# A mixer and mixture-of-experts kernel on one core: the final stage's roots of expert rows in two rounds of 8 and 24 tiles, and a new order of weighing and normalising

## The chip, the core and the metric

One core of a Trainium2 chip. The metric is device time in microseconds (us) of one execution, as the median of several runs; lower is better. The kernel before took 280.55 us in the median of 3 runs (280.05 to 281.44). Something the size of 0.5% (1.4 us) is about what a measurement of this kernel can tell from no change.

## The reference

The input x has 4096 tokens of 128 numbers. A gated state-space mixer and a layer norm come first; they lie outside the change. Then comes a mixture of 8 experts of which each token uses two, and a last layer norm:

```python
scores = xt @ gate_w
ew, ei = jax.lax.top_k(scores, K)          # K = 2
ew = jax.nn.softmax(ew, axis=-1)
h = gelu(einsum('td,edf->etf', xt, w1) + b1)
o = einsum('etf,efd->etd', h, w2) + b2
y = _layernorm(xt + o, ln_g, ln_b)         # per expert: (r - mean) * rsqrt(var + 1e-6) * g + b
out = einsum('et,etd->td', wE, y)          # two experts per token, with softmax weights
x = _layernorm(x + out)                    # eps 1e-5
```

## The kernel before

**Up to the final stage.** The kernel is written out by hand: each engine has its own instruction stream, and semaphores join them. After the mixer and the routing, every token is copied to the buckets of its two experts in device memory. 18 batches of 4 expert tiles go through TensorE, ScalarE (GELU) and VectorE. A row that leaves this part is (r - mean) * g with its mean and variance in two further columns (130 numbers), not yet multiplied by the root of the variance. GpSimd scatters the rows to `y_rows`, two per token.

**The final stage** starts when all scatters have landed. It handles 32 tiles of 128 tokens, in 8 groups of 4 tiles (g0 to g7), one PSUM bank for each group; two groups are a round (`ROUNDS` = 4, `OT` = 8 tiles). Its work on each engine is as follows.

- SP loads the expert rows of each group from `y_rows` into `yin` (L420; eight loads of 520 KB, all issued one after the other; the semaphore `yin_in[r]` is for round r). At the end it stores groups of the output as they become ready, g7 before g6 (L425).
- TensorE first adds up in each bank what needs no expert rows: the token itself (L778) and the weighted bias of the norm (L779), for all 8 groups. Then it adds, group by group in order, the token's first expert row (L783, two instructions in the profile of 512 columns; waits for `t0_ready`, which ScalarE gives for every 4 tiles) and its second expert row (L788, 8 instructions in the profile for 4 tiles of 128 columns; waits for `t1_ready`, which VectorE gives per tile). `sums_ready` counts the groups.
- VectorE `scales(r)`: the roots of the variances of a round, by shifts and three Newton steps, each of its 13 instructions waiting for the one before (`root_steps`): L1396, L1036, L1039, three times L1043, L1046, L1049, and L1401, which writes `scale`. A round has 8 tiles of 2 rows, so each instruction has 16 columns.
- VectorE `weigh_second(r)`: 8 multiplications of a 128x128 tile (L1411). ScalarE `weigh_first(r)`: the same for the first rows (L981). Both wait for the roots of their round.
- VectorE `second_statistics(r)`: 8 instructions that read the banks (L1420); wait for `sums_ready`.
- VectorE `second_norm_scales(r)`: the last norm's roots of a round, a chain of 14 steps and two closing instructions (L1013 to L1022, L1036 to L1049, L1433, L1434), 8 columns wide; gives `norm2_ready`.
- ScalarE `normalise_out(r)`: 8 tiles of the output (L989), waits for `norm2_ready`; of the last round it does 4 tiles and VectorE the other 4 (L1461).

**The order** on VectorE is written out by generators: one chain's next step is issued between two steps of another, so that its wait for its own predecessor is filled. It is `scales(0)` alone; `weigh_second(0)` with `scales(1)` between its tiles; the rest of `scales(1)`; `weigh_second(1)`; `second_statistics(0)`. Then, for r = 0 to 3, `second_norm_scales(r)` leads, and beside it run in this order `scales(r + 2)`, `weigh_second(r + 2)`, `second_statistics(r + 1)`, as far as these exist; what is left of them is issued behind. On ScalarE the order is `weigh_first` 0, 1, 2, `normalise_out(0)`, `weigh_first(3)`, `normalise_out` 1, 2, 3.

Of the kernel before, what the change touches and what calls it, by code (L numbers as in the profile page):

```python
# [2 lines left out]

# [6 lines left out]
ALU = mybir.AluOpType  # L10
# [3 lines left out]
P = 128  # L14
# [9 lines left out]
ROOT_STEPS = 13  # L24
# [43 lines left out]
def alone(steps):  # L68


    for _ in steps:
        pass


def later(k, n):

    return not isinstance(k, int) or k >= n


def mixer_moe_kernel(nc, x, W_u, b_u, W_g, b_g, A, Bm, Cm, D, gate_w, w1, b1, w2, b2, ln_g, ln_b, out):  # L80
# [16 lines left out]
    TOP = 2  # L97
# [7 lines left out]
    YW = DIM + 2  # L105
# [7 lines left out]
    ROUNDS = GROUPS // 2  # L113
    OT = 2 * TPG
# [14 lines left out]
    with ExitStack() as ctx:  # L129
        def sb(name, shape, dt=F32):  # L130
            return ctx.enter_context(nc.sbuf_tensor(name, shape, dt))

        def sem(name):
            return ctx.enter_context(nc.semaphore(name))
# [23 lines left out]
        rows = sb("rows", [ROWS, P])  # L158
# [29 lines left out]
        yin = by_token[:, 0:YIN].rearrange("p (a c) -> p a c", c=YW)  # L188
# [16 lines left out]
        weight = sb("weight", [P, TOP, GROUPS * TPG])  # L205
# [18 lines left out]
        zt = [z1T[i][:, 0:2 * P].rearrange("p (s d) -> p s d", d=P) for i in range(2)]  # L224
        stz = sb("stz", [P, BT, 6])
        yb = [powers_then_yb[:, i * BT * YW:(i + 1) * BT * YW].rearrange("p (s c) -> p s c", c=YW) for i in range(NB)]
        tmpz = sb("tmpz", [P, 6, OT * TOP])
        row_ids = [sb(f"row_ids{i}", [P, BT], I32) for i in range(NB)]
        tmp2 = sb("tmp2", [P, 6, OT])
        scale = sb("scale", [P, GROUPS * TPG, TOP])  # L230
# [71 lines left out]
        yin_in = [sem(f"yin_in{i}") for i in range(ROUNDS)]  # L302
        b2_steps = sem("b2_steps")
        root_steps = sem("root_steps")
# [14 lines left out]
        def block_of(s):  # L319

            return slice(s * P, (s + 1) * P)
# [471 lines left out]
        def _(act):  # L793
# [180 lines left out]

            def weigh_first(r):

                act.wait_ge(root_steps, (r + 1) * ROOT_STEPS)
                for j in range(OT):
                    t = r * OT + j
                    row = yin[:, t * TOP, 0:P]  # L980
                    ins = f(row, row, ACT.Copy, scale=scale[:, t, 0:1])  # L981
                    if j % TPG == TPG - 1:
                        ins.then_inc(t0_ready, 1)

            def normalise_out(r, tiles=OT):
                act.wait_ge(norm2_ready, r + 1)
                for j in range(tiles):
                    t = r * OT + j
                    ins = f(out_rows[:, t, :], bank[t // TPG][:, block_of(t % TPG)], ACT.Identity,  # L989
                            bias=nb2[:, t:t + 1], scale=rstd2[:, t:t + 1])  # L990
                    if j % TPG == TPG - 1:
                        ins.then_inc(out_ready, 1)

            weigh_first(0)
            weigh_first(1)
            for r in range(ROUNDS - 2):
                weigh_first(r + 2)
                normalise_out(r)
            normalise_out(ROUNDS - 2)
            normalise_out(ROUNDS - 1, TPG)  # L1000


# [1 line left out]
        def _(dve):  # L1004
            v = nc.vector
            cp, tt, ts, stt = v.tensor_copy, v.tensor_tensor, v.tensor_scalar, v.scalar_tensor_tensor

            def variance(steps, st, tmp, q, n, eps):

                me, mo, qe, qo = st[:, 0:n, 1], st[:, 0:n, 4], st[:, 0:n, 2], st[:, 0:n, 5]  # L1010
                d, dd = tmp[:, 0, 0:n], tmp[:, 2, 0:n]
                steps.wait()
                steps.step(tt(d, me, mo, ALU.subtract))  # L1013
                steps.step(tt(half_sums(tmp, n), me, mo, ALU.add))
                steps.step(tt(q, qe, qo, ALU.add))
                yield
                steps.wait()
                steps.step(stt(dd, d, 0.25, d, ALU.mult, ALU.mult))
                steps.step(ts(q, q, 1.0 / P, eps, ALU.mult, ALU.add))
                yield  # L1020
                steps.wait()
                steps.step(tt(q, q, dd, ALU.add))  # L1022
                yield

            def half_sums(tmp, n):
                return tmp[:, 1, 0:n]

            def root(tmp, n):
                return tmp[:, 5, 0:n]

            def rsqrt(steps, q, tmp, n):

                a, y = tmp[:, 4, 0:n], root(tmp, n)
                yi = y.bitcast(I32)
                steps.wait()
                steps.step(ts(yi, q.bitcast(I32), 1, None, ALU.logical_shift_right))  # L1036
                yield
                steps.wait()
                steps.step(ts(yi, yi, -1.0, float(RSQRT_MAGIC), ALU.mult, ALU.add))  # L1039
                yield  # L1040
                for _ in range(3):
                    steps.wait()
                    steps.step(tt(a, y, y, ALU.mult))  # L1043
                    yield
                    steps.wait()
                    steps.step(stt(a, a, -0.5, q, ALU.mult, ALU.mult))  # L1046
                    yield
                    steps.wait()
                    steps.step(stt(y, a, 1.5, y, ALU.add, ALU.mult))  # L1049
                    yield  # L1050
# [166 lines left out]
            rows_now, tiles, upto, one, taken_step, later_skip = (cnt[:, i, :] for i in range(6))  # L1217
# [170 lines left out]

            roots = Counted(dve, root_steps, ROOT_STEPS)

            def scales(r):

                dve.wait_ge(yin_in[r], 32)
                roots.open(r)
                roots.wait()
                roots.step(ts(tmpz[:, 3, :], yin[:, bass.ds(r * OT * TOP, OT * TOP), P + 1:YW]  # L1396
                              .rearrange("p j a -> p (j a)"), EPS_MOE, None, ALU.add))
                yield
                yield from rsqrt(roots, tmpz[:, 3, :], tmpz, OT * TOP)
                roots.wait()  # L1400
                roots.step(tt(scale[:, bass.ds(r * OT, OT), :], root(tmpz, OT * TOP).rearrange("p (j k) -> p j k", k=TOP),  # L1401
                              weight[:, :, bass.ds(r * OT, OT)].rearrange("p k j -> p j k"), ALU.mult))
                roots.close()

            def weigh_second(r):

                dve.wait_ge(root_steps, (r + 1) * ROOT_STEPS)
                for j in range(OT):
                    t = r * OT + j
                    row = yin[:, t * TOP + 1, 0:P]  # L1410
                    ts(row, row, scale[:, t, 1:2], None, ALU.mult).then_inc(t1_ready, 1)  # L1411
                    yield

            def second_statistics(r):
                if later(r, 1):
                    dve.wait_ge(out_steps, (r - 1) * OUT_STEPS + 3)
                for j in range(OT):
                    if j % TPG == 0:
                        dve.wait_ge(sums_ready, r * (OT // TPG) + j // TPG + 1)
                    ins = v.bn_stats(st2[:, j, :], bank[r * (OT // TPG) + j // TPG][:, block_of(j % TPG)])  # L1420
                    if j == OT - 1:
                        ins.then_inc(stats2_ready, 1)
                    yield

            def second_norm_scales(r):
                late.open(r)
                dve.wait_ge(stats2_ready, r + 1)
                if later(r, 1):
                    dve.wait_ge(norm2_ready, r)
                yield from variance(late, st2, tmp2, tmp2[:, 3, :], OT, EPS1)  # L1430
                yield from rsqrt(late, tmp2[:, 3, :], tmp2, OT)
                late.wait()
                late.step(cp(rstd2[:, bass.ds(r * OT, OT)], root(tmp2, OT)))  # L1433
                stt(nb2[:, bass.ds(r * OT, OT)], half_sums(tmp2, OT), -0.5, root(tmp2, OT), ALU.mult, ALU.mult)\  # L1434
                    .then_inc(norm2_ready, 1)
                late.close()

            alone(scales(0))
            second_scales = scales(1)
            for _ in weigh_second(0):  # L1440
                next(second_scales, None)
            alone(second_scales)
            alone(weigh_second(1))
            alone(second_statistics(0))
            for r in range(ROUNDS):


                beside = []
                if r + 2 < ROUNDS:
                    beside.append(scales(r + 2))  # L1450
                    beside.append(weigh_second(r + 2))
                if r + 1 < ROUNDS:
                    beside.append(second_statistics(r + 1))
                beside = chain(*beside)
                for _ in second_norm_scales(r):
                    next(beside, None)
                alone(beside)

            dve.wait_ge(norm2_ready, ROUNDS)
            for t in range((GROUPS - 1) * TPG, GROUPS * TPG):  # L1460
# [98 lines left out]
```

## Time and profile before

| | us |
|---|---|
| median of 3 runs | 280.55 |
| lowest, highest | 280.05, 281.44 |
| the profiled execution's own time | 280.12 |
| its span in the profile | 278.3 |
| TensorE matmul busy | 224.3 (81%) |
| VectorE busy | 173.6 (62%) |
| GpSimd busy | 139.8 (50%) |
| ScalarE busy | 137.7 (49%) |

All times of a trace count from the start of the span. The profiled execution took 1.82 us more than its span. A row of the timeline gives the start, the duration, the engine, the line in the kernel, what is written and read with the shapes, and how many instructions are merged in it; in brackets stands the idle time before it and who ended it. A row of merged instructions has the time from the first start to the last end. TensorE's granted clock (PEclk) is a share of 2.4 GHz: 1.00 is 2.4 GHz and 0.50 is 1.2 GHz. Idle time of an engine costs something only where the end of the kernel hangs on it, which the chain of waits shows.

### The profile page before, as it was taken

The page shows a single profiled execution, that of the slowest core. Times are in us where ns is not written, and L with a number is a line of the kernel's source. Part 1 is how long each engine was busy: PE and PEld are TensorE (multiplying, and loading weights), DVE is VectorE, ACT ScalarE, POOL GpSimd, SP SyncE. Part 2 cuts the span into 40 slices and gives each one's busy share as a digit, 9 for nine tenths or more (in the row PEclk, how much of TensorE's full clock was granted, in tenths as well). Part 3 has the DMA queues.
Part 4 walks back from the last instruction along what each step waited for, and adds up shares of the span by engine and source line. Part 5 has one row for each costly group of instructions (what it writes and reads, how often), then busy time and mean ns, then how long its engine had stood idle before and what let it go on. Part 6 is the DMA issues. An engine that isn't in the chain of part 4 may idle for free.

```text
span 278.3 us, 5571 instructions
## 1 busy us (share of the span) xinstructions
PE 224.3 (81%) x1316; PEld 169.5 (61%) x1317; DVE 173.6 (62%) x913; ACT 137.7 (49%) x404; POOL 139.8 (50%) x179
## 2 busy tenths in 40 slices
PE   3998998996798356447999999999999938997640
PEld 2476864664655335346888888888888823455330
DVE  1245527787628769475666676766666680569974
ACT  2242223667500304547667767776876500244844
POOL 7000000477777577777777777777777773000000
PEclk9999999999799777555999999999999986999895
DMA  5990000011111111644343333333232111940224
GB/s 170 293 273 14 0 0 1 21 50 61 48 57 38 38 58 55 150 103 117 86 106 98 102 102 107 84 107 96 81 93 64 58 38 33 419 164 1 75 75 151
DMA packets 22375, 25.66 MB, mean 92 GB/s; under 512 B 4388, under 2 KB 16569, under 8 KB 22348
## 3 DMA queue, kind: packets, MB, share of 16 engines
q1 hardware_dynamic: 17958, 16.84, 20.7%
q0 software_dynamic: 4352, 8.50, 9.2%
q8 instruction: 10, 0.16, 0.2%
q14 instruction: 17, 0.14, 0.2%
q10 hardware_dynamic: 38, 0.01, 0.0%
HBM read 14.15 MB, written 11.71 MB: 93 GB/s over the span
## 4 chain that ended last, share of the span: by engine, by line
PE 65%; DVE 21%; ACT 7%; issue 2%; DMA 1%; ACTq 1%; DVEq 0%
PE bank L721 14%; PE bank L731 13%; PE bank L733 4%; PE bank L455 3%; PE bank L778 3%; PE bank L456 3%; PE bank L779 3%; PE bank L474 3%; PE bank L706 3%; ACT pay L828 2%; PE bank L524 2%; PE bank L547 2%; PE bank L517 2%; PE bank L446 2%; PE bank L783 2%
## 5 line engine op out<-in xcount | busy, mean ns | idle before, releaser
L1516 POOL DMA_INDIRECT buckets<-pay,dest x64 | 63.2, 988 | 67.2 <-ACT pay L828 50.4
L1524 POOL DMA_INDIRECT y_rows<-powers_then_yb,row_ids x72 | 71.1, 987 | 24.5 <-issue 18.6
L731 PE MATMUL bank<-w_sb,hidden 128*128 x288 | 48.2, 290 | 0.0
L927 ACT ACTIVATE hidden<-bank,bcol 128x128 f32<-128x128 f32 x144 | 40.9, 371 | 9.7 <-PE bank L721 9.6
L721 PE MATMUL bank<-xbT,x_tok 128*128 128x128 f32 x288 | 44.1, 300 | 1.4 <-ACT xbT L909 1.4
L731 PEld LDWEIGHTS bank<-w_sb,hidden 128*128 128x128 f32 x288 | 38.1, 193 | 2.5
L721 PEld LDWEIGHTS bank<-xbT,x_tok 128*128 128x128 f32 x288 | 37.2, 202 | 4.0 <-ACT xbT L909 1.8
L917 ACT ACTIVATE x_tok<-w_sb 128x256 f32 x72 | 26.4, 432 | 0.7 <-issue 0.7
L1364 DVE SCALAR_TENSOR_TENSOR powers_then_yb<-z1T,powers_then_yb,gbc 128x128 f32<-128x128 f32 x72 | 22.2, 350 | 5.5 <-DVE powers_then_yb L1360 0.7
L828 ACT ACTIVATE pay<-z,nb,tmp 128x128 f32<-128x128 f32 x32 | 13.1, 484 | 24.2 <-DVE nb L1141 24.2
L1352 DVE TENSOR_TENSOR z1T<-bank,gates_then_xb 128x256 f32<-128x256 f32 x36 | 15.2, 421 | 13.0 <-PE bank L733 13.0
L981 ACT ACTIVATE by_token<-by_token,scale 128x128 f32<-128x128 f32 x32 | 9.8, 388 | 19.6 <-DVE scale L1401 19.6
L474 PE MATMUL bank<-by_token,powers_then_yb 128*128 128x128 f32 x60 | 14.3, 323 | 6.1 <-ACT by_token L817 4.2
L909 ACT ACTIVATE xbT<-bank 128x512 f32<-128x512 f32 x18 | 10.8, 599 | 16.8 <-PE bank L706 16.8
L1356 DVE BATCH_NORM_STATS2 stz<-z1T 128x6 f32<-128x128 f32 x72 | 17.5, 285 | 1.2
L733 PE MATMUL bank<-b_parts,ones 3*128 x72 | 16.2, 225 | 0.0
L474 PEld LDWEIGHTS bank<-by_token,powers_then_yb 128*128 128x128 f32 x60 | 9.8, 201 | 10.3 <-ACT by_token L817 6.8
L555 PE MATMUL bank<-chosen,before 128*128 128x32 bf16 x8 | 1.6, 197 | 17.5 <-DVE chosen L1189 17.5
L800 ACT ACTIVATE gates_then_xb<-bank,bcol 128x512 f32<-128x512 f32 x8 | 5.5, 687 | 17.5 <-PE bank L455 17.5
L547 PE MATMUL bank<-cat,z1T 128*128 128x136 f32 x64 | 12.2, 348 | 1.6 <-DVE z1T L1127 1.6
L547 PEld LDWEIGHTS bank<-cat,z1T 128*128 128x128 f32 x64 | 10.7, 242 | 4.0 <-DVE z1T L1127 3.0
L783 PE MATMUL bank<-by_token,cat 128*128 128x512 f32 x16 | 9.3, 668 | 4.6 <-ACT by_token L981 4.6
(187 smaller groups left out, 409.4 us busy)
## 6 DMA issues: line engine op xcount, KB each, us to landing
gates_then_xb<-buckets SPq DMA_DIRECT2D x72, 64.5 KB
by_token<-y_rows SPq DMA_DIRECT2D x8, 520.0 KB, 6.6
x_tok<-in_L_attn_x_dram SPq DMA_DIRECT2D x8, 256.0 KB, 5.5
out_dram<-out_rows SPq DMA_DIRECT2D x8, 256.0 KB, 2.5
y_rows<-powers_then_yb,row_ids POOLq DMA_INDIRECT x72, 2.3
w_sb<-in_L_ffn_w_dram SPq DMA_DIRECT2D x1, 1024.0 KB
buckets<-pay,dest POOLq DMA_INDIRECT x64, 2.3
buckets<-pad SPq DMA_DIRECT2D x9, 64.5 KB, 2.6
```

What stands on the lines that cost most here:

```text
L474: mm(ps_state[s % 2][:, 0:P], pq[:, 0, 1, :], local[h][:, block_of(s - 1)], start=False, stop=True).then_inc(state_product[h], 1)
L547: ins = mm(ps_tok[j // 2][:, c:c + CW], z1T[g % 2][:, block_of(j)], cat[:], start=True, stop=True)
L721: ins = mm(ps_hid[(q % 2) * 2 + h][:, at:at + P], w1_now[q][:, s, c * P:(c + 1) * P], xbT[q % 2][:, s, :], start=True, stop=True)
L731: mm(ps_o[h][:, i * P:(i + 1) * P], hidden[q % 2][:, s, c, :], w2_sb[:, bass.ds(e * (FC * P) + c * P, P)], start=(c == 0), stop=False)
L733: ins = mm(ps_o[h][:, i * P:(i + 1) * P], ones[0:PARTS, :], b2_parts[:, bass.ds(e * P, P)], start=False, stop=True)
L828: f(pay[0][:, g * TPG + j, 0:P], z1[g % 2][:, j, 0:P], ACT.Identity, bias=nb1[g % 2][:, j:j + 1], scale=tmp1[g % 2][:, 5, j:j + 1]).then_i ...
L917: ins = f(w1_now[q][:, s, :], w1_sb[:, bass.ds(e[s] * HID, HID)], ACT.Copy)
L927: ins = f(hidden[q % 2][:, s, c, :], ps_hid[(q % 2) * 2 + s // 2][:, at:at + P], ACT.Gelu, bias=bcol[:, bass.ds(e[s] * FC + BIAS_ROW + c, 1)])
L1356: ins = v.bn_stats(stz[:, s, :], buf[:, s - 2 * h, :])
L1364: stt(y[:, s, 0:P], buf[:, s - 2 * h, :], y[:, s, P:P + 1], gbc[:, bass.ds(e[s] * P, P)], ALU.subtract, ALU.mult).then_inc(yb_ready, 1)
L1516: pool.indirect_dma_start(buckets, bass.IndirectOffsetOnAxis(ap=dest[:, k, t:t + 1], axis=0), pay[k][:, t, :], None).then_inc(scattered[g ...
L1524: pool.indirect_dma_start(y_rows, bass.IndirectOffsetOnAxis(ap=row_ids[q][:, s:s + 1], axis=0), yb[q][:, s, :], None, bounds_check=TOKENS ...
```

## The change

On VectorE the roots of expert rows are made in two rounds: `scales(0, 0, 1)` for the first 8 tiles (16 columns), and `scales(1, 1, ROUNDS)` for the other 24 (48 columns), which waits for the loads of rounds 1 to 3 together. The second one leads, and `second_norm_scales(0)` runs beside it. So `weigh_second(1)` and the roots of round 1 come after `second_statistics(0)` instead of ahead of it, and `weigh_second(0)` has nothing beside it. `weigh_second(3)` runs beside `second_norm_scales(1)`, and `second_statistics(3)` beside `second_norm_scales(2)`, while `second_statistics` 1 and 2 stand alone.

On ScalarE the list is now written differently: `weigh_first` 0, 1, 2, `normalise_out(0)`, `weigh_first(3)`, `normalise_out` 1, 2, 3: `ROUNDS - 1` is 3, so it is the order of before, while `weigh_first` 1, 2 and 3 now all wait for the second round of roots. In detail:

```diff
--- before.py
+++ after.py
@@ -1,5 +1,4 @@
-from itertools import chain
...
@@ -224,7 +223,7 @@
         zt = [z1T[i][:, 0:2 * P].rearrange("p (s d) -> p s d", d=P) for i in range(2)]
         stz = sb("stz", [P, BT, 6])
         yb = [powers_then_yb[:, i * BT * YW:(i + 1) * BT * YW].rearrange("p (s c) -> p s c", c=YW) for i in range(NB)]
-        tmpz = sb("tmpz", [P, 6, OT * TOP])
+        tmpz = sb("tmpz", [P, 6, (ROUNDS - 1) * OT * TOP])
         row_ids = [sb(f"row_ids{i}", [P, BT], I32) for i in range(NB)]
         tmp2 = sb("tmp2", [P, 6, OT])
         scale = sb("scale", [P, GROUPS * TPG, TOP])
@@ -974,7 +973,7 @@
 
             def weigh_first(r):
 
-                act.wait_ge(root_steps, (r + 1) * ROOT_STEPS)
+                act.wait_ge(root_steps, min(r + 1, 2) * ROOT_STEPS)
                 for j in range(OT):
                     t = r * OT + j
                     row = yin[:, t * TOP, 0:P]
@@ -991,12 +990,12 @@
                     if j % TPG == TPG - 1:
                         ins.then_inc(out_ready, 1)
 
-            weigh_first(0)
-            weigh_first(1)
-            for r in range(ROUNDS - 2):
-                weigh_first(r + 2)
+            for r in range(ROUNDS - 1):
+                weigh_first(r)
+            normalise_out(0)
+            weigh_first(ROUNDS - 1)
+            for r in range(1, ROUNDS - 1):
                 normalise_out(r)
-            normalise_out(ROUNDS - 2)
             normalise_out(ROUNDS - 1, TPG)
 
 
@@ -1388,23 +1387,25 @@
 
             roots = Counted(dve, root_steps, ROOT_STEPS)
 
-            def scales(r):
-
-                dve.wait_ge(yin_in[r], 32)
-                roots.open(r)
+            def scales(n, first, last):
+
+                for r in range(first, last):
+                    dve.wait_ge(yin_in[r], 32)
+                tiles, rows = slice(first * OT, last * OT), (last - first) * OT * TOP
+                roots.open(n)
                 roots.wait()
-                roots.step(ts(tmpz[:, 3, :], yin[:, bass.ds(r * OT * TOP, OT * TOP), P + 1:YW]
+                roots.step(ts(tmpz[:, 3, 0:rows], yin[:, first * OT * TOP:last * OT * TOP, P + 1:YW]
                               .rearrange("p j a -> p (j a)"), EPS_MOE, None, ALU.add))
                 yield
-                yield from rsqrt(roots, tmpz[:, 3, :], tmpz, OT * TOP)
+                yield from rsqrt(roots, tmpz[:, 3, 0:rows], tmpz, rows)
                 roots.wait()
-                roots.step(tt(scale[:, bass.ds(r * OT, OT), :], root(tmpz, OT * TOP).rearrange("p (j k) -> p j k", k=TOP),
-                              weight[:, :, bass.ds(r * OT, OT)].rearrange("p k j -> p j k"), ALU.mult))
+                roots.step(tt(scale[:, tiles, :], root(tmpz, rows).rearrange("p (j k) -> p j k", k=TOP),
+                              weight[:, :, tiles].rearrange("p k j -> p j k"), ALU.mult))
                 roots.close()
 
             def weigh_second(r):
 
-                dve.wait_ge(root_steps, (r + 1) * ROOT_STEPS)
+                dve.wait_ge(root_steps, min(r + 1, 2) * ROOT_STEPS)
                 for j in range(OT):
                     t = r * OT + j
                     row = yin[:, t * TOP + 1, 0:P]
@@ -1435,26 +1436,22 @@
                     .then_inc(norm2_ready, 1)
                 late.close()
 
-            alone(scales(0))
-            second_scales = scales(1)
-            for _ in weigh_second(0):
-                next(second_scales, None)
-            alone(second_scales)
-            alone(weigh_second(1))
-            alone(second_statistics(0))
-            for r in range(ROUNDS):
-
-
-                beside = []
-                if r + 2 < ROUNDS:
-                    beside.append(scales(r + 2))
-                    beside.append(weigh_second(r + 2))
-                if r + 1 < ROUNDS:
-                    beside.append(second_statistics(r + 1))
-                beside = chain(*beside)
-                for _ in second_norm_scales(r):
+            def together(leading, beside):
+                for _ in leading:
                     next(beside, None)
                 alone(beside)
+
+            alone(scales(0, 0, 1))
+            alone(weigh_second(0))
+            alone(second_statistics(0))
+            together(scales(1, 1, ROUNDS), second_norm_scales(0))
+            alone(weigh_second(1))
+            alone(weigh_second(2))
+            alone(second_statistics(1))
+            together(second_norm_scales(1), weigh_second(3))
+            alone(second_statistics(2))
+            together(second_norm_scales(2), second_statistics(3))
+            alone(second_norm_scales(3))
 
             dve.wait_ge(norm2_ready, ROUNDS)
             for t in range((GROUPS - 1) * TPG, GROUPS * TPG):
```

## Rows read from the trace of the kernel before

**Rows 1.** The profile page, section 4: shares of the chain that ended last.
```profile
PE 65%; DVE 21%; ACT 7%; issue 2%; DMA 1%; ACTq 1%; DVEq 0%
```

**Rows 2.** Chain of waits: start us, us, engine, output, line, count.
```profile
260.64 1.28 ACT by_token L981 x4
...
261.97 2.08 PE bank L783 x2
264.05 1.41 PE bank L788 x8
...
266.31 0.91 PE bank L788 x8
```

**Rows 3.** Timeline of VectorE before 251 us: start, us, line, shapes, [idle before].
```profile
239.26 0.17 DVE L1396 TENSOR_SCALAR tmpz<-by_token 128x16 f32<-128x16 f32 x1 [9.50 <-DMA by_token<-y_rows]
...
245.37 1.66 DVE L1411 TENSOR_SCALAR by_token<-by_token,scale 128x128 f32<-128x128 f32 x8
248.39 0.89 DVE L1420 BATCH_NORM_STATS2 st<-bank 128x6 f32<-128x128 f32 x4 [1.35 <-PE bank L788]
```

**Rows 4.** Timeline of VectorE from 251 us on.
```profile
251.06 0.17 DVE L1013 TENSOR_TENSOR tmp<-st 128x8 f32<-128x8 f32 x1
...
253.88 0.17 DVE L1401 TENSOR_TENSOR scale<-tmpz,weight 128x16 f32<-128x16 f32 x1
...
254.64 0.16 DVE L1434 SCALAR_TENSOR_TENSOR nb<-tmp 128x8 f32<-128x8 f32 x1
...
262.44 1.67 DVE L1420 BATCH_NORM_STATS2 st<-bank 128x6 f32<-128x128 f32 x8
...
265.56 0.30 DVE L1420 BATCH_NORM_STATS2 st<-bank 128x6 f32<-128x128 f32 x1 [1.07 <-PE bank L788]
...
267.24 0.30 DVE L1420 BATCH_NORM_STATS2 st<-bank 128x6 f32<-128x128 f32 x1 [0.42 <-PE bank L788]
...
268.07 0.29 DVE L1420 BATCH_NORM_STATS2 st<-bank 128x6 f32<-128x128 f32 x1
...
269.54 0.16 DVE L1434 SCALAR_TENSOR_TENSOR nb<-tmp 128x8 f32<-128x8 f32 x1
...
273.13 1.36 DVE L1461 TENSOR_SCALAR out_rows<-bank,rstd,nb 128x128 f32<-128x128 f32 x4
```

**Rows 5.** The two SP rows of the loads: timeline, and time from issue to landing.
```profile
234.34 3.83 SPq L420 DMA_DIRECT2D by_token<-y_rows  x8
...
DMA to landing us min/median/max: 3.6/6.6/9.7
```

**Rows 6.** Groups of VectorE instructions by shape: busy us, mean ns of one, idle.
```profile
L1204 DVE TENSOR_TENSOR sel<-picked,sel 128x32 f32<-128x32 f32 x16 | 2.4, 190 | 0.3
...
L1043 DVE TENSOR_TENSOR tmpz<-tmpz 128x16 f32<-128x16 f32 x12 | 2.1, 174 | 0.1
```

**Rows 7.** Timeline of TensorE, final stage.
```profile
249.05 1.05 PE L788 MATMUL bank<-by_token,cat 128*128 128x128 f32 x8
...
255.43 1.13 PE L783 MATMUL bank<-by_token,cat 128*128 128x512 f32 x2 [1.82 <-ACT by_token L981]
...
258.14 1.05 PE L788 MATMUL bank<-by_token,cat 128*128 128x128 f32 x8
```

**Rows 8.** Busy by stretch: from:to, length, each engine's busy us, PEclk, DMA, GB/s.
```profile
261.60:261.80 0.20, 0.00 (x0) 0.00 (x0) 0.20 (x2) 0.20 (x2) 0.00 (x0) 0.50 0.00 0
...
264.50:265.00 0.50, 0.50 (x4) 0.50 (x4) 0.00 (x0) 0.50 (x2) 0.00 (x0) 0.50 0.00 0
265.00:265.50 0.50, 0.50 (x5) 0.48 (x5) 0.00 (x0) 0.50 (x3) 0.00 (x0) 0.99 0.34 131
...
271.00:272.00 1.00, 0.00 (x0) 0.00 (x0) 0.83 (x6) 1.00 (x4) 0.00 (x0) 0.92 0.00 0
```

**Rows 9.** Timeline of ScalarE, final stage.
```profile
245.37 2.45 ACT L981 ACTIVATE by_token<-by_token,scale 128x128 f32<-128x128 f32 x8 [0.95 <-DVE scale L1401]
...
256.45 2.87 ACT L989 ACTIVATE out_rows<-bank,nb,rstd 128x128 f32<-128x128 f32 x8
```

## The prediction

> **What bounds the kernel now.** The page comes first: the chain that ended last is 65% TensorE and 21% VectorE [rows 1]. The change touches only what follows the last expert batch, so I read the chain of waits from there on. It shows a stage in which three engines take turns: ScalarE weighs four tiles, TensorE adds g6 and g7, VectorE takes their statistics and makes the roots [rows 2]. The timelines then give the price of each turn. VectorE waits for the first loads until 239.26, and works from 251.06 to 273.13 with two short idles of 1.07 and 0.42 us, both for TensorE [rows 3, 4]. So after 251 us the end hangs on VectorE's own list, and on TensorE where it is late. Ahead of 251.06 VectorE has room: TensorE is still adding what needs no expert rows, and VectorE idles 1.35 us before the first statistics [rows 3].
>
> **Up to 251.06: nothing gained or lost.** The first roots start at the same 239.26. The second round of roots (13 instructions) and 8 weighings leave this stretch. They lay in front of the idle of 1.35 us, which gets longer; `second_statistics(0)` waits for TensorE's g0 and g1, and g1 ends at 250.10 (249.05 + 1.05) either way [rows 3, 7]. This takes work out of a hole and puts it where VectorE is the bound.
>
> **The wait for all loads** costs nothing: the eight are issued by 238.17 and the slowest takes 9.7 us to land, so all are there before 248, three microseconds ahead of the first instruction that waits [rows 5]. SP's stores keep their order, and nothing else is queued on SP behind them. GpSimd has nothing here.
>
> **The wide roots, 251.06 to 254.3.** Before, 13 steps of 16 columns beside a norm chain took 2.99 us (251.06 to 253.88 + 0.17) [rows 4]. No row has this operation at 48 columns. The nearest: 190 ns at 32 columns and 174 at 16 [rows 6], so 16 ns for 16 columns and 32 for the 32 added. Bounds are 0 (the link's latency hides it) and 0.1 us each (three times the slope). I take 0.03: 13 x 0.03 = 0.4. The roots lead now instead of coming after the first three norm instructions, which gives back about 0.1. They end at 251.06 + 2.99 + 0.4 - 0.1 = 254.3 (253.9 to 255.3 by the bounds). The norm chain beside them ends 0.9 us behind the roots' last start before (254.80 against 253.88) [rows 4], so near 255.0 now; VectorE can begin to weigh at 254.8, between its last steps.
>
> **Round 1's turn, the term that decides.** ScalarE starts round 1 at 254.3 instead of in the early hole (245.37) [rows 9]. Four tiles take 1.28 [rows 2], so TensorE can start g2 at 255.6. It had finished g1 at 250.10: it stands idle 5.5 us. In the run before it went on with g2 and g3 at once. What does it do after an idle? After 1.82 us it ran at full clock [rows 7]. After the end of g5 at 259.19 the granted clock was 0.50 from 261.6 on, 2.4 us later, and g6 ran at half clock, 2.08 + 1.41 = 3.49 us; it was back at 0.99 from 265.0 [rows 2, 7, 8]. After the last matmul of all, at 267.2, the fall came inside 271 to 272 us (mean 0.92), so 4.6 us later [rows 8]. An idle of 5.5 us is longer than both, so I take half clock for g2, at the price of g6: 3.49, and then 1.77 for g3 at full clock (as g7, 265.45 to 267.22) [rows 2]. g3 ends at 255.6 + 3.49 + 1.77 = 260.9. VectorE takes its 4 statistics in 0.04 + 0.89 [rows 3] and is done at 261.8.
>
> The Trainium skill, page TensorE: Matmul & The Clock Gate, Part 1, says that the number of slow matmuls at a kernel's start differs from run to run of the same kernel. By it the time would lie anywhere between those of the first two rivals, 280.6 and 284.1; one trace of one execution can't confirm it.
>
> **VectorE's own list meanwhile**: 16 weighings from 254.8 at 1.66 for 8 [rows 3] until 258.1, then 8 statistics of 1.70 [rows 4] until 259.8, if TensorE were never late. So the half clock costs 2.0 us here. The move of round 1 alone is covered by what the change saves elsewhere, as the next rival shows.
>
> **The rest, from 261.8.**
> - Norm chain 1 with `weigh_second(3)` beside it. A chain alone takes 3.43 (269.70 to 273.13, at 0.20 a step); with a tile of 128 columns beside a step the pair takes 0.28 (267.24 to 268.07 is three pairs) [rows 4]. 3.43 + 8 x 0.08 = 4.07. The other reading is norm chain 2 before: 264.11 to 269.70 less the idles 1.07 and 0.42 is 4.10, and the idles hide a little more. I take 4.0 (3.8 to 4.2): 265.8.
> - `second_statistics(2)` alone, 1.70: 267.5. TensorE has had g4 and g5 since 264.5 (260.9 + two times 1.77), so there is no wait.
> - Norm chain 2 with the last statistics, 4.0: 271.5. Those need g6 and g7: ScalarE weighs rounds 1 and 2, normalises round 0 and weighs g6 by 254.3 + 2 x 2.45 + 2.87 + 1.28 = 263.4 [rows 2, 9], before TensorE is free at 264.5, so g7 ends near 268.0. Its first statistic is due at about 268.9. The two idles of before are gone.
> - Norm chain 3 alone, 3.43: 274.9, where it was 273.13.
> - The tail (four tiles on each engine, and the stores of g7 and g6) is the same work in the same spacing; it moves as a whole.
>
> **ScalarE** is no bound: its work from 254.3 is three weighings of 2.45, three normalisings of 2.87 and half of one, 17.4 us, so it could be done at 271.7, and it starts its last half at 274.9.
>
> **The sum.** 274.9 - 273.13 = +1.8 us. The profiled execution took 280.12, so 281.9; the median is 0.43 above it, so 282.3.
>
> **Rivals.**
> - *Not slower: TensorE is at full clock for g2, or its slow stretch is hidden.* Then g3 ends at 255.6 + 2 x 1.77 = 259.1, its statistics at 260.0, and 4.0 + 1.7 + 4.0 + 3.43 behind it give 273.2: +0.1, 280.6. It decides if the clock is still full when g2 starts at 255.6. For it speaks the clock that held for 4.6 us after the last matmul; against it the 5.5 us, and the fall after 2.4. Here also belongs a smaller price of the list (wide roots free, chains at 3.8), with a half-length slow stretch. Together 0.27.
> - *The half clock lasts through g2 and g3.* Both at twice 1.77 take 7.1: g3 ends at 262.7 instead of 260.9: +3.6, 284.1. The one slow stretch near it in the trace ended 3.0 us after TensorE's start (261.97 to 265.0), less than this needs; 0.13.
> - *Faster: VectorE is bound by the number of its instructions.* After 251.06 there are 13 fewer root instructions (26 become 13): 13 x 0.174 = 2.26 saved, plus 1.49 of idle that goes; against it 1.66 for `weigh_second(1)` and 0.4 for the width. -1.7 with TensorE never late: 278.9. Against it: norm chain 0 with 13 roots beside it took 3.74 (251.06 to 254.80), only 0.3 more than a chain alone [rows 4], so the roots lay in gaps and their removal saves 0.3 a round. 0.07. The Trainium skill, page VectorE: DVE Perf Modes, section on the TRN2 errata, would have it this way: a fixed cost for each instruction from SBUF, so few wide ones are cheaper than many narrow ones. The rows agree on the cost of one (174 ns for 16 columns, 190 for 32) and not on what it is worth here.
>
> **How the numbers follow.** My case has 0.53, with its own range 281.2 to 283.2: about 0.40 of it lies above 281.95 (0.5% over the median), 0.13 within. The long half clock adds 0.13 to slower. The first rival's 0.27 goes to same (0.25) but for 0.02 above the bound, and the third is faster. So slower is 0.40 + 0.13 + 0.02 = 0.55, same 0.13 + 0.25 = 0.38, faster 0.07. The likeliest time is 282.3. The range runs from the full-clock case less a few tenths for the free width (280.3) to the long half clock (284.0).
>
> **What would show it in the profile.** Idle of VectorE ahead of the first statistics near 4.7 us instead of 1.35; the wide roots at about 0.20 us each, ending at 254.3; the granted clock at 0.50 when g2 starts at 255.6, and VectorE idle for TensorE before the statistics of g2 and g3, together about 2 us; no idle before the last statistics; the last norm chain alone at 3.43 ending near 274.9. The prediction is wrong if the clock is full at 255.6, if the roots end after 255.3, or if a norm chain with eight tiles beside it takes well under 3.8.

## The result, and the profile after

The changed kernel took 285.49 us in the median of 4 runs (283.80 to 286.06); the kernel before took 281.0 beside it (280.05 to 282.60). The ratio is 1.0183, 95% interval 1.0126 to 1.0239: slower, by more than the 282.3 forecast and outside its range of 280.3 to 284.0. A second comparison of the unedited kernel, in the first experiment below, gave 1.0131 (1.0078 to 1.0185). The ratios leave out executions more than 1.5% above the fastest of their kernel, the medians do not.

| | before | after |
|---|---|---|
| the profiled execution's own time | 280.12 | 283.80 |
| its span | 278.3 | 282.1 |
| first root instruction starts | 239.26 | 240.28 |
| last four tiles on VectorE start | 273.13 | 276.91 |
| between them, "the stage" below | 33.87 | 36.63 |
| VectorE busy | 173.6 | 171.4 |

VectorE is busy 2.2 us less (26 instructions fewer) and the end comes later. The timeline of VectorE in the kernel after has the rows that answer to [rows 3, 4]:

```profile
240.28 0.17 DVE L1397 TENSOR_SCALAR tmpz<-by_token 128x16 f32<-128x16 f32 x1 [9.78 <-DMA by_token<-y_rows]
...
249.16 0.89 DVE L1421 BATCH_NORM_STATS2 st<-bank 128x6 f32<-128x128 f32 x4 [4.50 <-PE bank L787]
250.91 0.89 DVE L1421 BATCH_NORM_STATS2 st<-bank 128x6 f32<-128x128 f32 x4 [0.86 <-PE bank L787]
251.72 0.18 DVE L1397 TENSOR_SCALAR tmpz<-by_token 128x48 f32<-128x48 f32 x1
...
254.75 0.21 DVE L1402 TENSOR_TENSOR scale<-tmpz,weight 128x48 f32<-128x48 f32 x1
...
255.43 3.22 DVE L1412 TENSOR_SCALAR by_token<-by_token,scale 128x128 f32<-128x128 f32 x16
260.21 0.89 DVE L1421 BATCH_NORM_STATS2 st<-bank 128x6 f32<-128x128 f32 x4 [1.56 <-PE bank L787]
263.07 0.89 DVE L1421 BATCH_NORM_STATS2 st<-bank 128x6 f32<-128x128 f32 x4 [1.97 <-PE bank L787]
264.00 0.17 DVE L1012 TENSOR_TENSOR tmp<-st 128x8 f32<-128x8 f32 x1
...
267.78 1.67 DVE L1421 BATCH_NORM_STATS2 st<-bank 128x6 f32<-128x128 f32 x8
269.49 0.17 DVE L1012 TENSOR_TENSOR tmp<-st 128x8 f32<-128x8 f32 x1
...
273.32 0.16 DVE L1435 SCALAR_TENSOR_TENSOR nb<-tmp 128x8 f32<-128x8 f32 x1
```

The two idles of 1.07 and 0.42 us before the last statistics are gone. In their place stand 1.56 and 1.97 us before those of g2 and g3. What VectorE waits for there is TensorE; its timeline (compare [rows 7]), and the busy table by stretch around its slow part (columns as in [rows 8]):

```profile
249.81 1.05 PE L787 MATMUL bank<-by_token,cat 128*128 128x128 f32 x8
256.33 2.07 PE L782 MATMUL bank<-by_token,cat 128*128 128x512 f32 x2 [5.46 <-ACT by_token L980]
258.19 1.91 PE L787 MATMUL bank<-by_token,cat 128*128 128x128 f32 x8
259.90 1.92 PE L782 MATMUL bank<-by_token,cat 128*128 128x512 f32 x2
261.61 1.43 PE L787 MATMUL bank<-by_token,cat 128*128 128x128 f32 x8
262.87 1.02 PE L782 MATMUL bank<-by_token,cat 128*128 128x512 f32 x2
```

```profile
255.25:255.50 0.25, 0.00 (x0) 0.00 (x0) 0.22 (x3) 0.25 (x2) 0.00 (x0) 1.00 0.00 0
255.50:255.75 0.25, 0.00 (x0) 0.00 (x0) 0.25 (x3) 0.25 (x2) 0.00 (x0) 0.61 0.00 0
...
262.00:262.25 0.25, 0.25 (x4) 0.25 (x2) 0.00 (x0) 0.25 (x2) 0.00 (x0) 0.50 0.79 303
262.25:262.50 0.25, 0.25 (x3) 0.25 (x3) 0.00 (x0) 0.25 (x2) 0.00 (x0) 0.73 1.03 393
```

TensorE stood idle for 5.46 us. The granted clock fell to 1.2 GHz near 255.55 (mean 0.61 in the quarter of a microsecond from 255.50), 0.8 us before g2 could start, and came back near 262.4. So g2 (to 260.1, by the chain of waits) and nearly all of g3 (to 263.05) ran at half clock: 6.72 us for the two, where two groups at full clock take 3.5.

Behind the first statistics (from 251.06 before, 251.72 after) the last tiles come 22.07 and 25.19 us later: +3.12. VectorE's waits for TensorE make 2.04 of it (1.56 + 1.97 against 1.07 + 0.42), and its own list is 1.08 longer.

### The profile page after: what moved, and what is told of

It is laid out like the page before. It is cut to its first block, busy times and chain, and to the rows that moved or that the text cites. A ratio compares the mean times of both kernels' runs of the same rounds, so it can differ in the third digit from the quotient of the medians.

```text
span 282.1 us, 5542 instructions
## 1 busy us (share of the span) xinstructions
PE 223.9 (79%) x1314; PEld 168.8 (60%) x1317; DVE 171.4 (61%) x887; ACT 137.4 (49%) x404; POOL 140.2 (50%) x179
## 3 DMA queue, kind: packets, MB, share of 16 engines
HBM read 14.15 MB, written 11.71 MB: 92 GB/s over the span
## 4 chain that ended last, share of the span: by engine, by line
PE 65%; DVE 22%; ACT 7%; issue 3%; DMA 1%; ACTq 1%; DVEq 0%
PE bank L720 13%; PE bank L730 13%; PE bank L732 4%; PE bank L454 3%; PE bank L777 3%; PE bank L473 3%; PE bank L455 3%; PE bank L778 3%; PE bank L705 2%; ACT pay L827 2%; PE bank L523 2%; PE bank L782 2%; PE bank L546 2%; PE bank L516 2%; PE bank L787 2%
## 5 line engine op out<-in xcount | busy, mean ns | idle before, releaser
L782 PE MATMUL bank<-by_token,cat 128*128 128x512 f32 x16 | 10.1, 720 | 5.5 <-ACT by_token L980 5.5
L988 ACT ACTIVATE out_rows<-bank,nb,rstd 128x128 f32<-128x128 f32 x28 | 10.2, 461 | 6.2 <-DVE nb L1435 6.2
```

## The experiments

Theory A: the time is TensorE at half clock after the idle. Theory B: it is VectorE's own list, longer by the wide roots and the order. The stage of each kernel, from the traces. Its start hangs on the landing of the loads and the first statistics on TensorE, so its first part varies: 11.44 and 11.78 us in the two traces of the changed kernel, 11.80 and 11.71 in those of the kernel before. The next column leaves that part out: it counts from the end of the first statistics to the last four tiles.

| kernel | median us | ratio to before (95%) | stage us | behind the first statistics, us | half clock beside g2 to g7, us |
|---|---|---|---|---|---|
| before, its two traces | 281.0 to 281.8 | 1 | 33.87, 33.83 | 22.07, 22.12 | 3.4 (g6) |
| changed, its two traces | 285.49, 285.03 | 1.018, 1.013 | 36.63, 36.98 | 25.19, 25.20 | 6.8 (g2, g3) |
| e2_after_filled | 281.85 | 0.9998 (0.9959 to 1.0037) | 33.80 | 22.29 | none |
| f2_after_half_filled | 283.69 | 1.0122 (1.0067 to 1.0176) | 36.42 | 25.21 | 6.8 |
| g1_after_bridge | 282.99 | 1.0040 (1.0002 to 1.0079) | 35.38 | 23.58 | 3.4 (g2) |
| f4_late_narrow | 285.24 | 1.0134 (1.0086 to 1.0183) | 36.51 | 24.95 | 6.8 |
| e4_before_filled | 279.03 | 0.9886 (0.9828 to 0.9944) | 32.32 | 20.63 | none |
| e3_round1_back | 278.97 | 0.9901 (0.9868 to 0.9934) | 31.60 | 19.74 | none |
| f3_round1_back_early_fill | 277.64 | 0.9786 (0.9711 to 0.9861) | 29.80 | 19.75 | none |

### The changed kernel again (e1_after_again)

No edit.

> The changed kernel once more, unedited, in five rounds. Theory A (half clock: TensorE idles 5.5 us before g2 and then runs g2 and most of g3 at 1.2 GHz): again slower by 4 to 5.5 us, with the granted clock at 0.50 when g2 starts and VectorE idle before the statistics of g2 and g3 for 1.5 to 3.5 us; executions with a lower mean clock are the longer ones. Theory B (VectorE's own list is longer, by the wide roots and the new order): slower by the same in all executions, whatever the mean clock.

Measured: slower by 1.31%, 3.7 us (4 to 5.5 was expected); the traced execution had the same picture: idles of 1.56 and 1.96 us before the statistics of g2 and g3, and half clock from 256.3 to 263.1. The mean clock of the six executions lies between 0.887 and 0.898 and the shortest two (283.31, 283.75) have 0.898, the longest (286.11) 0.887. That goes with A but does not tell it from B: the executions of the kernel before show the same (279.15 us at 0.920, the four of 284.00 to 284.75 at 0.883 to 0.898). The trace says more: the stage is 36.98, and 25.20 us lie behind the first statistics, as in the first trace.

### TensorE kept busy in the idle (e2_after_filled)

In short form; the matmuls add zeros to g7's bank and change no number:

```diff
 for g in range(GROUPS):
+    if g == 2:
+        for _ in range(22):
+            mm(bank[GROUPS - 1][:], before[:], table16[:], start=False, stop=False)
     pe.wait_ge(t0_ready, g + 1)
```

> The changed kernel with 22 matmuls of 512 columns of zeros (bfloat16) that TensorE adds to the last bank between g1 and g2, about 4.7 us at full clock in the idle of 5.5 us; they change no number. Theory A: g2 and g3 run at full clock (1.75 us each instead of 3.5 and 3.3), the idle before their statistics falls to under 0.5 us, and the time comes down by 3 to 4.5 us against the changed kernel, to 280 to 282. Theory B: the time stays within 1 us of the changed kernel's.

```profile
252.82 4.91 PE L782 MATMUL bank<-table,before 128*128 128x512 bf16 x22
258.45 1.12 PE L787 MATMUL bank<-by_token,cat 128*128 128x512 f32 x2 [0.72 <-ACT by_token L985]
259.41 1.05 PE L792 MATMUL bank<-by_token,cat 128*128 128x128 f32 x8
```

```profile
257.55 3.22 DVE L1417 TENSOR_SCALAR by_token<-by_token,scale 128x128 f32<-128x128 f32 x16
260.69 0.88 DVE L1426 BATCH_NORM_STATS2 st<-bank 128x6 f32<-128x128 f32 x4
262.26 0.89 DVE L1426 BATCH_NORM_STATS2 st<-bank 128x6 f32<-128x128 f32 x4 [0.68 <-PE bank L792]
```

These are timelines of TensorE and of VectorE. The pair of 512 columns takes 1.12 instead of 2.07 us, the idle before the statistics of g2 is gone and 0.68 stays before g3's (under 0.5 was expected). The median came down by 3.2 us against the changed kernel's 285.03, and the ratio to before is 0.9998. The stage is 33.80: 2.83 and 3.18 us under the two traces of the changed kernel. VectorE's list is the same in both, so B falls as the cause of these 3 us. It also shows the change at full clock to be worth nothing against the kernel before, which still has its own slow g6.

### Round 1 back in the early hole (e3_round1_back)

```diff
-alone(weigh_second(0))
-alone(second_statistics(0))
-together(scales(1, 1, ROUNDS), second_norm_scales(0))
-alone(weigh_second(1))
+together(weigh_second(0), scales(1, 1, 2))
+alone(weigh_second(1))
+alone(second_statistics(0))
+together(scales(2, 2, ROUNDS), second_norm_scales(0))
 alone(weigh_second(2))
```

The two waits for `root_steps` count three rounds of roots here (not shown).

> The changed kernel with round 1's roots and weighing put back ahead of the first statistics, so three rounds of roots of 8, 8 and 16 tiles; the last round (32 columns) leads beside the first norm chain, and the rest of the new order stays. Theory A: TensorE has g2 and g3 done by 254, its idle before g4 is about 1.8 us and before g6 about 1.5, so the clock stays full; by the durations of the two traces the last norm chain ends about 2 us before that of the kernel before: 278 to 280. Theory B: merging two narrow rounds into a wide one and the new order cost as much here, 282 or more.

```profile
257.21 1.13 PE L782 MATMUL bank<-by_token,cat 128*128 128x512 f32 x2 [1.79 <-ACT by_token L980]
...
262.32 1.13 PE L782 MATMUL bank<-by_token,cat 128*128 128x512 f32 x2 [1.33 <-ACT by_token L980]
```

TensorE's idles are 1.79 before g4 and 1.33 before g6, and it stays at full clock (1.13 for the pair). The stage is 31.60, 2.2 us under before's, as expected, and the median 278.97. A merged round of roots and the new order do no harm; the place of round 1 does. Against the kernel before at full clock (e4, the next run) they even shorten VectorE's list by 0.89 us behind the first statistics (20.63 to 19.74), though the medians of the two are alike (279.03, 278.97).

### The kernel before, with its own idle filled (e4_before_filled)

The edit of e2 on the kernel before, with 11 matmuls and `g == 6`.

> The kernel before with 11 matmuls of zeros between g5 and g6, about 2.4 us in its idle of 2.8 us. Theory A: g6 and g7 run at full clock, the two idles of VectorE before the last statistics (1.07 and 0.42 us) go, and the time falls by 1 to 1.6 us, to about 279.3. Theory B, and any theory by which TensorE's clock does not reach the end: no change within 0.5 us.

```profile
263.38 1.13 PE L788 MATMUL bank<-by_token,cat 128*128 128x512 f32 x2 [0.41 <-ACT by_token L986]
```

The pair of g6 takes 1.13 instead of 2.08 us. The stage is 32.32, 1.55 us under before's, and VectorE has no idle before the last statistics. So even the kernel before paid for a slow g6. By whole times the gain is 1.14% (3.2 us, interval 1.6 to 4.8), more than the stage shows at its middle.

### A second trace of the kernel before (f1_before_again)

No edit.

> The kernel before once more, for a second trace of it. If the execution in the first trace was typical, the stage from the first root instruction to the last four tiles takes 33.9 us again, with g6 at half clock. If the first trace was a lucky one, so that the prediction was summed from a wrong base, the stage is over 34.5 us or the first roots start well after 239.3.

```profile
241.27 0.17 DVE L1396 TENSOR_SCALAR tmpz<-by_token 128x16 f32<-128x16 f32 x1 [9.68 <-DMA by_token<-y_rows]
...
267.51 0.30 DVE L1420 BATCH_NORM_STATS2 st<-bank 128x6 f32<-128x128 f32 x1 [1.11 <-PE bank L788]
...
275.10 1.37 DVE L1461 TENSOR_SCALAR out_rows<-bank,rstd,nb 128x128 f32<-128x128 f32 x4
```

The stage is 33.83 against 33.87, with the idles of before within 0.1 us. But it starts 2.0 us later than in the first trace (241.27, in [rows 3] 239.26), and the execution took 282.11. Both halves of the expectation came true: the stage was a typical one, the base under it was not.

### Half of the filling (f2_after_half_filled)

As e2, with 11 matmuls instead of 22.

> The changed kernel with 11 matmuls of zeros right behind g1, so TensorE's idle before g2 is about 3.0 us instead of 5.5. Theory A1 (the length of the slow stretch follows from the length of the idle, so an idle of 3 us costs what one of 2.8 us cost in the kernel before): half clock for about 3 us, g2 slow and g3 fast, time 1 to 1.7 us below the changed kernel's. Theory A2 (any idle in which the clock falls costs the long stretch): g2 and most of g3 slow as before, no gain. Theory A3 (the clock does not fall, as the idle ends before the fall came in the traces of the changed kernel): full clock, 3 us below.

```profile
255.59 2.07 PE L787 MATMUL bank<-by_token,cat 128*128 128x512 f32 x2 [3.09 <-ACT by_token L985]
257.46 1.91 PE L792 MATMUL bank<-by_token,cat 128*128 128x128 f32 x8
```

An idle of 3.09 us gave g2 the same 2.07 + 1.91 us as one of 5.46, and half clock from 254.8 to 261.6. The kernel before, after an idle of 2.77, had 3.4 us of it. A2 holds in the trace; A1 and A3 fall. Behind the first statistics the gain is nothing (25.21 against 25.19 and 25.20). The median is 1.3 us lower, but the ratio to before, 1.0122, is that of the changed kernel (1.0131) within both intervals.

### Round 1 late, but narrow roots (f4_late_narrow)

```diff
-together(scales(1, 1, ROUNDS), second_norm_scales(0))
-alone(weigh_second(1))
-alone(weigh_second(2))
+together(scales(1, 1, 2), second_norm_scales(0))
+together(weigh_second(1), scales(2, 2, 3))
+together(weigh_second(2), scales(3, 3, 4))
 alone(second_statistics(1))
```

The two waits for `root_steps` count four rounds again (not shown).

> The changed kernel with its roots again in four rounds of 8 tiles (16 columns), but round 1's roots and weighing still behind the first statistics: the roots of round 1 lead beside the first norm chain, those of rounds 2 and 3 run beside the weighings of rounds 1 and 2. Theory A (the late start of round 1 is what costs, not the width): TensorE idles over 5 us before g2 and g2 is slow again, time 284 to 287. Theory B (the wide rounds cost): the time comes back to that of the kernel before, within 1 us.

```profile
258.42 2.08 PE L782 MATMUL bank<-by_token,cat 128*128 128x512 f32 x2 [5.12 <-ACT by_token L980]
```

```profile
264.21 0.88 DVE L1421 BATCH_NORM_STATS2 st<-bank 128x6 f32<-128x128 f32 x4
265.24 0.89 DVE L1421 BATCH_NORM_STATS2 st<-bank 128x6 f32<-128x128 f32 x4 [0.15 <-PE bank L787]
```

The median is 285.24 and the stage 36.51, near the changed kernel's. The width of the roots does not make TensorE's idle; the late start of round 1 does. The time is a weaker proof than it looks. VectorE waits only 0.15 us for the slow groups here, where the changed kernel waits 3.53, because its own list is 3.1 us longer: 8 weighings with 13 narrow roots between them take 3.40 us (257.52 to 260.92), while the changed kernel's 16 weighings alone take 3.22. So the half clock is hidden behind that list, and at full clock this kernel would gain about 0.15 us (an estimate from that wait). That a wide round costs little by itself is shown by its 3.24 us and by e3.

### A bridge of four matmuls (g1_after_bridge)

```diff
+    if g == 2:
+        pe.wait_ge(root_steps, 2 * ROOT_STEPS)
+        for _ in range(4):
+            mm(bank[GROUPS - 1][:], before[:], table16[:], start=False, stop=False)
     pe.wait_ge(t0_ready, g + 1)
```

> The changed kernel with 4 matmuls of zeros that TensorE starts when the wide roots are done, about 1.3 us before g2 can start; they fill 0.9 us of those. In the traces so far the half clock lasted 3.4 us where TensorE restarted 0.2 to 0.3 us after the fall, and 6.8 us where it restarted 0.5 to 0.7 us after it. Theory A4 (the restart's place against the fall decides the length): here TensorE works from 0.7 us ahead of the place of the fall, so the half clock lasts 3.4 us or does not come; g3 at full clock, VectorE's two idles before the statistics of g2 and g3 fall from 3.5 us together to under 2, stage from first root to last tiles 35.3 us or less instead of 36.6 to 37.0, the time 1.3 us or more below the changed kernel's. Rival (the long idle before decides, 4 us of it remain): half clock of 6.8 us as before, no gain.

```profile
256.41 1.11 PE L784 MATMUL bank<-table,before 128*128 128x512 bf16 x3 [4.38 <-DVE scale L1406]
257.49 2.07 PE L786 MATMUL bank<-by_token,cat 128*128 128x512 f32 x2
259.36 1.46 PE L791 MATMUL bank<-by_token,cat 128*128 128x128 f32 x8
260.66 1.02 PE L786 MATMUL bank<-by_token,cat 128*128 128x512 f32 x2
```

The first row shows 3 of the 4 matmuls; one has no record. TensorE had been at work for 0.4 us when the clock fell near 256.8, and the clock was back near 260.2: 3.4 us of half clock, g2 slow and g3 fast. VectorE's two idles are 1.11 and 0.79, the stage is 35.38 (35.3 or less was expected), 1.25 and 1.60 us under the changed kernel's, and behind the first statistics 1.6 under; the median is 2.0 under. The idle before the bridge was still 4.38 us, longer than the whole one of f2. So the length of the idle does not decide between the short and the long stretch. The place of the restart against the fall goes with it in all seven traces that have one, and this run, made to test that, came out as forecast. The restart came 0.3 to 0.4 us after the fall in the short cases and 0.6 to 0.8 us in the long ones; the expectation has both about 0.1 us too small.

### The best version (f3_round1_back_early_fill)

The version of e3 and, behind the last expert batch:

```diff
+pe.wait_ge(xbT_ready, BATCHES)
+for _ in range(19):
+    mm(bank[5][:], before[:], table16[:], start=True, stop=True)
 pe.wait_ge(wE_ready, 1)
```

> The version with round 1 back in the early hole (roots of 8, 8 and 16 tiles), and 19 matmuls of zeros in TensorE's idle of 4.6 us behind the last expert batch. Theory A: the clock stays full through the sums that need no expert rows, which now begin with two slow pairs; g0 ends up to 2 us earlier, VectorE's idle before the first statistics (1.5 and 0.86 us) shrinks, and the time falls by 1 to 2 us more, to about 277. The rival: those sums lie beside the loads of the expert rows, and nothing changes at the end (within 0.5 us).

```profile
226.88 4.05 PE L764 MATMUL bank<-table,before 128*128 128x512 bf16 x18 [0.16 <-issue]
231.28 0.44 PE L767 MATMUL bank<-cat,wE 128*128 128x128 f32 x2 [0.34 <-DVE wE L1386]
232.19 1.13 PE L780 MATMUL bank<-pay,cat 128*128 128x512 f32 x2 [0.47 <-ACT wET L973]
```

The first row shows 18 of the 19 matmuls. The sums that need no expert rows begin with 1.13 us for a pair instead of 2.08, and VectorE's idle before the first statistics goes (0.67 us before g1's stays). The stage is 29.80, 1.8 us under e3's, all of it ahead of the end of the first statistics (10.05 against 11.86 us), and the median 277.64, 1.3 under. It is the fastest kernel of the study: 2.1% under the kernel before (1.4 to 2.9) by a ratio that rests on three of its six executions, 1.3% by the medians of all.

## Why the prediction was wrong

The direction and the mechanism were right, and the decisive term was mis-sized. Step by step, counted from the end of the first statistics (251.06 before, 251.72 after):

- *Up to the first statistics*: nothing of the change there, as forecast; VectorE's idle grew from 1.35 to 4.50 us (forecast 4.7). The 1.0 us by which the loads land later in the trace of after is no effect of the change: in the kernel before's second trace they land 2.0 later.
- *The wide roots*: forecast 3.24 us, measured 254.96 - 251.72 = 3.24, at 0.24 us a link.
- *TensorE's idle and g2's start*: forecast 5.5 us and 4.5 us behind the reference point; measured 5.46 and 4.61.
- ***Round 1's turn* is the step that failed.** I priced it by g6: 3.49 us for a slow g2 and 1.77 for a fast g3, together 5.26, with half clock for 3.0 us of TensorE's work. It took 3.78 + 2.94 = 6.72, with 6.1 us of slow work, and VectorE waited 3.53 us for the two groups where I had about 2. The rival of the long half clock held (0.13); my range ended a tenth below its own 284.1. I argued against it with the only slow stretch near it in the trace, one draw, and of a kind that depends on where the work restarts. The trace had a longer one which I didn't use: after the last expert batch the clock was at half from 227.5 to 234.3.
- *Chains with tiles beside them*: forecast 4.0 each, measured 3.87 (264.00 to 267.87) and 3.99 (269.49 to 273.48). The 8 statistics alone 1.7, the last chain 3.43, no idle between: as forecast.
- *The sum of the stage*: +1.8 forecast; +3.12 measured behind the first statistics in both traces (25.19 and 25.20 against 22.07). With the clock full in g2 and g3 my first rival had +0.1, and e2 has +0.2 (22.29), so the rest of the sum came out right.
- *The base.* The profiled execution began the stage at 239.26, and over the ten other traces the first root starts at 239.77 to 242.58, whatever the kernel. That start goes with the time TensorE spent at half clock ahead of 225 us (summed over windows of 1 us): 30.7 to 34.1 us in the three traces that start at 239.26 to 240.28, 37.5 or 37.6 in the six that start at 240.48 to 241.27, 41.0 and 44.4 in the two that start after 242.3. The same kernel has 34.1 and 37.5 in its two traces, so this differs from execution to execution; that it causes the later start is not shown. In the larger samples the kernel before has medians of 281.27 to 281.8, not 280.55. That is about 1 us of the miss of 3.2; the mis-sized term is 1.3. The remaining 0.9, which is the first comparison's 5.1 us (interval 3.5 to 6.7) against the stage's 3, stays open; the second comparison, 3.7 us with an interval from 2.2 to 5.2, holds the stage's.

The experiments take the +3.1 us behind the first statistics apart. Half clock in g2 and g3 costs 2.9 (25.20 in the changed kernel, 22.29 in e2). At full clock in both, the change itself costs 22.29 - 20.63 = 1.66 (e2 against e4): round 1's work moved out of a hole. The kernel before's slow g6, which the change removes, gives 1.44 back (22.07 against 20.63).

The Trainium skill's rule of a fixed cost for each instruction from SBUF (page VectorE: DVE Perf Modes, section on the TRN2 errata) was a rival for "faster". The 26 instructions fewer are there in the busy time, and the change is slower all the same. What such instructions are worth hangs on what stands beside them: 13 fewer, with the new order, go with a list shorter by 0.89 us in e3, and f4's narrow rounds between the weighings with one longer by 3.1.

The Trainium skill, page TensorE: Matmul & The Clock Gate, section Why this matters for your kernels, advises against long TensorE idles between bursts of matmuls. The traces agree: in the final stage every idle of 2.77 us or more was followed by half clock (in g1_after_bridge from 0.4 us after the restart), and none of 1.82 us or less was.

## What to carry to other kernels

Work in front of a wait that looks like idle time may be what keeps another engine running: before moving it, work out the other engine's new idle, and price its restart by the longest slow stretch in the trace, not by the nearest. Where a restart can't be avoided, matmuls of zeros into an open sum (e2, e4) or into a bank not yet in use (f3) keep the clock at full in a wait, and a few that begin before the clock falls already halve the loss (g1: 1.6 of 2.9 us). Measure from an event inside the stage: counted from the end of the first statistics each kernel's two traces agree within 0.05 us, while the whole times of the two executions of the kernel before differed by 2.0, and the changed kernel's stage, counted from its first root, by 0.35. And look whether an experiment's time comes from the cause it was made for: f4's did not.

## What the runs showed of the hardware

- Half clock came in two lengths in the final stage: 3.4 us in before, its repetition and g1, 6.8 us in the four traces with the long one. In the short cases TensorE restarted 0.3 to 0.4 us after the fall (before, its repetition) or was at work (g1), in the long ones 0.6 to 0.8 us after it. Why these few tenths decide is open.
- The fall came 2.2 to 4.8 us after the last matmul ahead of the idle, so the idle's length alone did not tell when it would come: 2.4 us in the kernel before behind g5, 4.7 in the changed one behind g1. No run has an idle between 1.82 and 2.77 us in that stage.
- Tripling the columns of a dependent VectorE instruction from 16 to 48 raised the link from 0.21 to 0.24 us.
